# The normalization of three token groups in the first expert stage: on ScalarE instead of VectorE

## The chip, the cores and the metric

The kernel runs on one core of a Trainium2 chip. The metric is the device time of one execution in microseconds (us), the median over the runs. Below, PE is TensorE, DVE VectorE, ACT ScalarE, POOL GpSimd and SP SyncE, the names that the profile uses.

## What is computed

There are 16 sequences of 128 tokens with 128 features and a context of 77 rows per sequence. Four residual layers follow each other, each on the layer-normalized state:

```
x = x + tanh(g_xattn[0]) * attention(layernorm(x), ctx)            # one head
x = x + tanh(g_ffn[0])   * experts16(layernorm(x))  # top 4 of 16, and a shared one
x = x + tanh(g_xattn[1]) * attention(layernorm(x), ctx)            # 16 heads of 8
x = x + tanh(g_ffn[1])   * experts8(layernorm(x))   # top 2 of 8
layernorm(x) = (x - mean(x)) / sqrt(var(x) + 1e-5)
```

An expert is `silu(x @ gate) * (x @ up)`, weighted with the token's share for this expert, times a down matrix.

## The kernel before

All tokens lie in SBUF as `X`, token in the partition. The work runs over NG = 4 groups of GB = 4 sequences (GT = 512 tokens); a layer goes through the groups one after another, and a layer's first group is prepared inside the layer before it. I call the layers the set-up stage (with the first attention), the first expert stage (`mB`), the attention stage (`c_body`) and the last expert stage (`mD`). Every engine has its own program, written out in order by hand, and they meet only at semaphores.

To normalize a group, DVE takes the statistics of four sequences (`norm_stats`, L1043: `bn_stats` into `st`, `bn_aggr` into `mv`, then `ve` = variance + EPS at L1052). POOL raises `ve` to the power -1/2 (`inv_std`, L335: `rstd`). Then `norm_apply` writes `xn` = (X - mean) * rstd, one instruction per sequence; in the first expert stage and the last one DVE does it (L1054, L1059), in the attention stage POOL (L399, L404 and L407). The set-up stage has a form of its own: POOL also makes `shiftA` = -mean * rstd (L346), with `lessA` = -mean from DVE (L1084), and for three of its groups ACT writes `xn` as scale * X + bias (L832). PE transposes `xn` into the bank `Tb` (`norm_T`, L478), ACT copies it out as the high part `xh` (`norm_hi`, L822), and DVE subtracts the two for the low part `xl` (`norm_lo`, L1063).

Each expert stage has 8 units per group (`m.units`; in the first one a unit is two experts). For unit k of group g:

- PE (`m_up`, L551) computes gate and up in six matmuls into `S` banks. It runs two units ahead, and unit k waits until DVE has gated unit k-2 (L553, semaphore `t2`). `m_down` (L559) multiplies the weighted hidden rows `hb` by the down matrix.
- ACT (`m_silu`, L854) makes `sg` = silu(gate). It waits for PE's gate and for DVE's weighted unit k-2.
- DVE (`m_gated`, L1195) multiplies `sg` by up, and (`m_weighted`, L1200) by the tokens' weights `CR`, giving `hb`.
- SP (`weight_rows`, L294) writes the router's weights to memory once per group and loads them back, spread over the partitions, into a ring `CR` of four slots.

Around these units the bodies place the rest: in PE's body, for k = 0 the transposes of the next group, for k = 1 its router matmuls (L588, L589); in ACT's body `norm_hi` at k = 2 of the program (L902), the copy of the layer's result `ysb` at k = 1, and DMA issues of value pieces after each silu; in DVE's body (`m_body`, L1213) the router's steps at k = 2 to 5, `norm_stats` of the group after the next at k = 6 (L1243), and `norm_apply` of it at k = 7 (L1245). In the first expert stage this last call is made for three groups. DVE's program for groups 1 and 2 is a loop (L1317), ACT's is written out (L951). POOL's part of the stage is `inv_std` three times, at L434, L435 and L439; `split_up` (the up weights into high and low) and `expand_keys` for the attention stage stand behind the second and the third.

Of the kernel before, what the change touches and what calls it, by code (L numbers as in the profile page):

```python
# [79 lines left out]
def flamingo(nc, x, ctxT, ctx, w0, w4, gate_router, w13, w2, up, down, consts, out, comb_rows):  # L80
    with ExitStack() as stack:
        at = [16512]

        def sb(name, shape, dt=F32, offset=None):

            size = 4
            for n in shape[1:]:
                size *= n
            if offset is None:
                offset = at[0]  # L90
                at[0] += -(-size // 32) * 32
            place[name] = offset
            return nc.alloc_sbuf_tensor_at(name, shape, dt, offset=offset)
# [62 lines left out]
        mv = sb("mv", [P, GB, 2])  # L156
        ve = sb("ve", [P, GB])
        rstd = sb("rstd", [P, GB])
        mvA = sb("mvA", [P, 2, GB, 2])
        veA = sb("veA", [P, 2, GB])  # L160
        lessA = sb("lessA", [P, 2, GB])
# [57 lines left out]
        vs_zero, vx_rdy, wo_rdy = sem("vs_zero"), sem("vx_rdy"), sem("wo_rdy")  # L219
        sh_up, sh_silu, sh_hid, sh_hi, sh_lo = map(sem, ("sh_up", "sh_silu", "sh_hid", "sh_hi", "sh_lo"))  # L220
        w2s_hi, w2s_lo = sem("w2s_hi"), sem("w2s_lo")
        up_split, centred = sem("up_split"), sem("centred")
        stored = sem("stored")

# [100 lines left out]
        def _(pool):  # L325
# [9 lines left out]
            def inv_std(n):  # L335
                pool.wait_ge(var_rdy, n)
                nc.gpsimd.tensor_tensor(rstd[:], ve[:], mhalf[:], ALU.pow).then_inc(rstd_rdy, 1)  # L337

            def inv_stdA(n):
                par = n % 2  # L340
                pool.wait_ge(varA, n)
                if n > 2:
                    pool.wait_ge(xn_rdy, n - 2)
                nc.gpsimd.tensor_tensor(rstdA[:, par], veA[:, par], mhalf[:], ALU.pow).then_inc(powA, 1)
                wait_apart(pool, powA, n)
                nc.gpsimd.tensor_tensor(shiftA[:, par], lessA[:, par], rstdA[:, par], ALU.mult).then_inc(rstdA_rdy, 1)  # L346
# [84 lines left out]
                        inv_std(2 * NG + 3 + g)  # L431
                        norm_apply(2 * NG + 3 + g, (g + 2) % NG)

            inv_std(NG + 3)  # L434
            inv_std(NG + 4)  # L435
            pool.wait_ge(in_up, 96)
            for n in range(NG):
                split_up(n)
            inv_std(2 * NG + 1)  # L439
            pool.wait_ge(k_l, NG)  # L440
            expand_keys(0, 0, first=True)
            expand_keys(1, 1, first=True)
# [360 lines left out]
        def _(act):  # L803
# [46 lines left out]
            def keys_hi(g):  # L850
                act.wait_ge(k_mm, g + 1)
                A(kh[:, g * GS:(g + 1) * GS], bK[g][:, 0:GS], ACT.Identity, bias=cols[:, 2:3]).then_inc(k_h, 1)

            def m_silu(m, g, k):  # L854
                act.wait_ge(m.g_done, m.units * g + k + 1)
                if used(g, k):
                    act.wait_ge(m.h_done, START + m.units * g + k - 1)
                A(sg[:, k % 2, :], Gb[k % 2][:], ACT.Silu).then_inc(m.s_done, 1)  # L858
# [23 lines left out]
            def m_body(m, g, nxt, then=None, begun=0):  # L882

                for k in range(m.units):
                    if k >= begun:
                        m_silu(m, g, k)
                    if then:
                        then(k)
                    if k == 1 and used(g, 0):
                        m_y_copy(m, g - 1)  # L890
                    if k == 2 and m.shared:
                        act.wait_ge(sh_up, g + 1)
                        if used(g, 0):
                            act.wait_ge(sh_lo, g)
                        A(hs[:], Eb[64:P, :], ACT.Silu).then_inc(sh_silu, 1)
                    if k == 3 and m.shared:
                        act.wait_ge(sh_hid, g + 1)
                        if used(g, 0):
                            act.wait_ge(m.dn, START + m.units * (g - 1) + 5)
                        A(hst[0:64, :], hs[:], ACT.Copy).then_inc(sh_hi, 1)  # L900
                    if nxt is not None and k == 2:
                        norm_hi(nxt[0], xh[:, bass.ds(slot(nxt[2]), GT)])  # L902
                    if nxt is not None and nxt[1] is not None and k == 3:
                        m_route_act(nxt[1], nxt[2])
                    if nxt is not None and nxt[1] is not None and k == m.units - 3:
                        m_route_tanh(nxt[1], nxt[2])
                    if nxt is not None and nxt[1] is not None and k == m.units - 2:
                        m_route_copy(nxt[1], nxt[2])

            norm_hi(1, xf[:, 0])  # L910
            score_weights(2)
# [120 lines left out]
        def _(dve):  # L1032
# [10 lines left out]
            def norm_stats(n, g):  # L1043
                for t in range(GB):
                    i = V.bn_stats(st[:, t, :], xt(g, t))
                i.then_inc(stats, 1)
                wait_apart(dve, stats, n)
                for t in range(GB):
                    i = V.bn_aggr(mv[:, t, :], st[:, t, :])
                i.then_inc(aggr, 1)  # L1050
                dve.wait_ge(aggr, n)
                V.tensor_scalar(ve[:], mv[:, :, 1], EPS, None, ALU.add).then_inc(var_rdy, 1)  # L1052

            def norm_apply(n, g, first=False):  # L1054
# [158 lines left out]
            def m_body(m, g, nxt, then=None, stats_of=None, apply_next=True, begun=0):  # L1213

                for k in range(m.units):
# [26 lines left out]
                        route_weights(nm, ng)  # L1242
                    if stats_of is not None and k == m.units - 2:  # L1243
                        norm_stats(n + 1, stats_of)
                    if stats_of is not None and apply_next and k == m.units - 1:  # L1245
                        norm_apply(n + 1, stats_of)
                if then:
                    then(m.units)
# [229 lines left out]
```

## Time and profile before

| | |
|---|---|
| median of 3 runs | 322.72 us (322.35 to 323.2) |
| the profiled execution | 322.1 us, span 320.3 us |
| mean granted TensorE clock in it | 0.987 |
| PE, DVE, ACT, POOL busy | 89%, 74%, 41%, 27% of the span |
| instructions | 5453 |

The span is the time from the first to the last instruction of the core; the execution's own time also holds what lies around it. Busy shares are averages over all stages. The chain that ended last is followed back from the last instruction, at each step to what released it. In a timeline, a number in brackets is the time for which the engine had nothing to do ahead of the instruction, and behind the arrow stands what ended it.

### The profile page before, as it was taken

The page shows a single profiled execution, that of the slowest core. Times are in us where ns is not written, and L with a number is a line of the kernel's source. Part 1 is how long each engine was busy: PE and PEld are TensorE (multiplying, and loading weights), DVE is VectorE, ACT ScalarE, POOL GpSimd, SP SyncE. Part 2 cuts the span into 40 slices and gives each one's busy share as a digit, 9 for nine tenths or more (in the row PEclk, how much of TensorE's full clock was granted, in tenths as well). Part 3 has the DMA queues.
Part 4 walks back from the last instruction along what each step waited for, and adds up shares of the span by engine and source line. Part 5 has one row for each costly group of instructions (what it writes and reads, how often), then busy time and mean ns, then how long its engine had stood idle before and what let it go on. Part 6 is the DMA issues. An engine that isn't in the chain of part 4 may idle for free.

```text
span 320.3 us, 5453 instructions
## 1 busy us (share of the span) xinstructions
PE 283.6 (89%) x1646; PEld 210.7 (66%) x1646; DVE 237.1 (74%) x660; ACT 129.9 (41%) x275; POOL 87.7 (27%) x162
## 2 busy tenths in 40 slices
PE   6899689999899799488789789889889999999994
PEld 5688467666476465277677677768676676676661
DVE  2887979769989986557677686686748977778572
ACT  1587533242342332445454554554442332323320
POOL 8475310100650410733175165355110100100000
PEclk9999979999999999889999999999999999999999
DMA  6900164282341430000000000000024053231640
GB/s 225 337 21 0 37 222 148 54 242 67 102 156 46 132 123 33 0 2 0 2 1 2 0 2 3 0 0 3 0 86 158 25 190 75 106 125 35 210 154 33
DMA packets 15066, 25.26 MB, mean 79 GB/s; under 512 B 2341, under 2 KB 4339, under 8 KB 14835
## 3 DMA queue, kind: packets, MB, share of 16 engines
q1 hardware_dynamic: 12968, 23.88, 22.6%
q10 hardware_dynamic: 2072, 1.07, 1.2%
q8 instruction: 13, 0.21, 0.3%
q14 instruction: 13, 0.11, 0.1%
HBM read 22.98 MB, written 1.25 MB: 76 GB/s over the span
## 4 chain that ended last, share of the span: by engine, by line
PE 65%; issue 10%; DVE 9%; ACT 5%; DMA 5%; POOL 3%; SPq 2%; POOLq 0%; DVEq 0%; ACTq 0%
PE S L542 24%; PE Ybank L564 15%; PE Ybank L710 10%; PE S L687 2%; PE Tb L482 2%; DMA CR<-comb_rows 2%; DMA X<-in_x 2%; PE bank L697 2%; DVE xn L1059 2%; DMA comb_rows<-ct 1%; ACT pt L973 1%; PE Tb L674 1%; ACT PX L963 1%; SPq L307 1%; PE bank L580 1%
## 5 line engine op out<-in xcount | busy, mean ns | idle before, releaser
L858 ACT ACTIVATE sg<-S 128x512 f32<-128x512 f32 x64 | 38.0, 596 | 72.5 <-PE S L542 62.6
L1205 DVE TENSOR_TENSOR hb<-sg,CR 128x512 f32<-128x512 f32 x64 | 45.1, 705 | 13.0 <-issue 4.8
L337 POOL TENSOR_TENSOR rstd<-ve,mhalf 128x4 f32<-128x4 f32 x11 | 11.1, 1011 | 134.6 <-DVE ve L1052 134.6
L1198 DVE TENSOR_TENSOR sg<-sg,S 128x512 f32<-128x512 f32 x64 | 43.5, 680 | 5.7 <-ACT sg L858 3.5
L710 PE MATMUL Ybank<-VX,pt 128*128 128x128 f32 (+1 forms) x320 | 39.1, 277 | 6.7 <-ACT pt L973 6.7
L710 PEld LDWEIGHTS Ybank<-VX,pt 128*128 128x128 f32 (+1 forms) x320 | 37.1, 191 | 9.2 <-issue 9.1
L542 PE MATMUL S<-xh,WBH 128*128 128x512 f32 x64 | 33.3, 520 | 5.8 <-DVE sg L1198 3.0
L542 PE MATMUL S<-xh,UPH 128*128 128x512 f32 x64 | 36.1, 565 | 0.0
L564 PE MATMUL Ybank<-hb,W2T 128*128 128x512 f32 x64 | 33.0, 599 | 1.6 <-DVE hb L1205 1.6
L564 PE MATMUL Ybank<-hb,downw 128*128 128x512 f32 x64 | 33.0, 599 | 0.4 <-DVE hb L1205 0.4
L973 ACT ACTIVATE pt<-bank 128x512 f32<-128x512 f32 (+1 forms) x32 | 15.8, 494 | 35.4 <-PE bank L697 35.4
L1334 DVE TENSOR_REDUCE cmx<-S 128x8 f32<-128x616 f32 x32 | 25.4, 794 | 6.1 <-PE S L687 6.1
L963 ACT ACTIVATE PX<-PX 128x616 f32<-128x616 f32 x32 | 23.0, 720 | 11.3 <-DVE PX L1342 11.2
L1342 DVE TENSOR_TENSOR PX<-S,cmx 128x616 f32<-128x616 f32 x32 | 25.6, 800 | 1.1
L542 PE MATMUL S<-xh,WBL 128*128 128x512 f32 x64 | 25.5, 398 | 0.0
L542 PE MATMUL S<-xl,WBH 128*128 128x512 f32 x64 | 25.3, 395 | 0.0
L542 PE MATMUL S<-xh,UPL 128*128 128x512 f32 x64 | 25.2, 394 | 0.0
L542 PE MATMUL S<-xl,UPH 128*128 128x512 f32 x64 | 25.0, 391 | 0.0
L418 POOL COPY VX<-VS 128x36 f32 (+3 forms) x80 | 13.7, 220 | 41.0 <-PE Ybank L710 33.2
L542 PEld LDWEIGHTS S<-xh,WBH 128*128 128x128 f32 x64 | 12.0, 188 | 16.2 <-DVE sg L1198 9.0
L354 POOL TENSOR_TENSOR KT<-kk,CB 128x616 fp32r<-128x616 f32 x16 | 19.7, 1233 | 2.0 <-PE S L687 1.8
L542 PEld LDWEIGHTS S<-xl,UPH 128*128 128x128 f32 x64 | 12.1, 189 | 7.7 <-issue 6.2
(164 smaller groups left out, 513.2 us busy)
## 6 DMA issues: line engine op xcount, KB each, us to landing
CR<-comb_rows SPq DMA_DIRECT2D x64, 128.0 KB, 3.0
CR<-comb_rows SPq DMA_DIRECT2D x32, 256.0 KB, 3.5
w13raw<-in_w SPq DMA_DIRECT2D x1, 1088.0 KB, 10.9
X<-in_x SPq DMA_DIRECT2D x4, 256.0 KB, 6.1
upraw<-in_up SPq DMA_DIRECT2D x4, 256.0 KB, 3.9
out_x<-X SPq DMA_DIRECT2D x4, 256.0 KB, 3.4
cT<-in_ctxT SPq DMA_DIRECT2D x2, 308.0 KB, 5.6
CN<-in_ctx SPq DMA_DIRECT2D x1, 616.0 KB
```

Of the source, the lines that this page charges most:

```text
L354: nc.gpsimd.tensor_tensor(KT[:, par].rearrange("p a (h k) -> p a h k", h=HG), keys, heads, ALU.mult).then_inc(ks_done, 1)
L418: i = nc.gpsimd.tensor_copy(dst[:, :, j, h * HV:(h + m) * HV].rearrange("p u (i d) -> p u i d", i=m), src[:, :, j, 0:m])
L542: i = mm(dst, wp[:, col:col + P], xp[:, bass.ds(xs, GT)], start=n == 0, stop=n == 2)
L564: mm(Ybank[:, bass.ds(slot(g), GT)], m.wd[:, k, :], hb[:, k % 2, :], start=k == 0, stop=k == m.units - 1, skip_group_check=True).then_inc( ...
L710: i = mm(bO9[c // CU], pt[0:w, t % 2, c * P:(c + 1) * P], VX[0:w, t % 2, c, :], start=c % CU == 0, stop=c % CU == CU - 1)
L858: A(sg[:, k % 2, :], Gb[k % 2][:], ACT.Silu).then_inc(m.s_done, 1)
L963: A(p, p, ACT.Exp).then_inc(c_exp, 1)
L973: A(pt[:, t % 2, 4 * r * P:4 * r * P + w], bPa[r][:, 0:w], ACT.Copy).then_inc(c_ev, 1)
L1198: V.tensor_tensor(sg[:, k % 2, :], sg[:, k % 2, :], Ub[k % 2][:], ALU.mult).then_inc(m.t2, 1)
L1205: V.tensor_tensor(hb[:, k % 2, :], sg[:, k % 2, :], CR[:, k % RING, :], ALU.mult).then_inc(m.h_done, 1)
L1334: V.tensor_reduce(cmx[:, 2 * u:2 * u + 2, :], pair(u), AX, ALU.max, negate=True).then_inc(c_mx, 1)
L1342: V.tensor_tensor(PX[:, t % 2, u * UK:(u + 1) * UK].rearrange("p (s h k) -> p s h k", s=2, h=HG), pair(u), cmx[:, 2 * u:2 * u + 2, :].unsq ...
```

## The change

DVE's `norm_stats` also writes `less` = -mean. For three groups POOL forms `shift` = `less` * `rstd` behind the power (`inv_std_shift`). ACT's new `norm_applyB` writes `xn` as scale * X + bias in four activations, behind the silu of unit 7 and ahead of the silu of the next group's unit 0. DVE's `norm_apply` stays in the last expert stage only, and for the first stage's first transition (L1304), which is called apart.

```diff
--- before.py
+++ after.py
@@ -156,6 +156,8 @@
         mv = sb("mv", [P, GB, 2])
         ve = sb("ve", [P, GB])
         rstd = sb("rstd", [P, GB])
+        less = sb("less", [P, GB])
+        shift = sb("shift", [P, GB])
         mvA = sb("mvA", [P, 2, GB, 2])
         veA = sb("veA", [P, 2, GB])
         lessA = sb("lessA", [P, 2, GB])
@@ -219,6 +221,7 @@
         vs_zero, vx_rdy, wo_rdy = sem("vs_zero"), sem("vx_rdy"), sem("wo_rdy")
         sh_up, sh_silu, sh_hid, sh_hi, sh_lo = map(sem, ("sh_up", "sh_silu", "sh_hid", "sh_hi", "sh_lo"))
         w2s_hi, w2s_lo = sem("w2s_hi"), sem("w2s_lo")
+        shift_rdy = sem("shift_rdy")
         up_split, centred = sem("up_split"), sem("centred")
         stored = sem("stored")
 
@@ -335,6 +338,11 @@
             def inv_std(n):
                 pool.wait_ge(var_rdy, n)
                 nc.gpsimd.tensor_tensor(rstd[:], ve[:], mhalf[:], ALU.pow).then_inc(rstd_rdy, 1)
+
+            def inv_std_shift(n):
+                inv_std(n)
+                wait_apart(pool, rstd_rdy, n)
+                nc.gpsimd.tensor_tensor(shift[:], less[:], rstd[:], ALU.mult).then_inc(shift_rdy, 1)
 
             def inv_stdA(n):
                 par = n % 2
@@ -431,12 +439,12 @@
                         inv_std(2 * NG + 3 + g)
                         norm_apply(2 * NG + 3 + g, (g + 2) % NG)
 
-            inv_std(NG + 3)
-            inv_std(NG + 4)
+            inv_std_shift(NG + 3)
+            inv_std_shift(NG + 4)
             pool.wait_ge(in_up, 96)
             for n in range(NG):
                 split_up(n)
-            inv_std(2 * NG + 1)
+            inv_std_shift(2 * NG + 1)
             pool.wait_ge(k_l, NG)
             expand_keys(0, 0, first=True)
             expand_keys(1, 1, first=True)
@@ -851,6 +859,14 @@
                 act.wait_ge(k_mm, g + 1)
                 A(kh[:, g * GS:(g + 1) * GS], bK[g][:, 0:GS], ACT.Identity, bias=cols[:, 2:3]).then_inc(k_h, 1)
 
+            def norm_applyB(n, g):
+                act.wait_ge(shift_rdy, n - NG - 2)
+                act.wait_ge(xnT, n - 1)
+                for t in range(GB):
+                    i = A(xn[:, t * P:(t + 1) * P], X[:, g * GT + t * P:g * GT + (t + 1) * P], ACT.Identity,
+                          bias=shift[:, t:t + 1], scale=rstd[:, t:t + 1])
+                i.then_inc(xn_rdy, 1)
+
             def m_silu(m, g, k):
                 act.wait_ge(m.g_done, m.units * g + k + 1)
                 if used(g, k):
@@ -906,6 +922,8 @@
                         m_route_tanh(nxt[1], nxt[2])
                     if nxt is not None and nxt[1] is not None and k == m.units - 2:
                         m_route_copy(nxt[1], nxt[2])
+                    if nxt is not None and nxt[1] is mB and k == m.units - 1:
+                        norm_applyB(nxt[0] + 1, (nxt[2] + 1) % NG)
 
             norm_hi(1, xf[:, 0])
             score_weights(2)
@@ -1049,6 +1067,7 @@
                     i = V.bn_aggr(mv[:, t, :], st[:, t, :])
                 i.then_inc(aggr, 1)
                 dve.wait_ge(aggr, n)
+                V.tensor_scalar(less[:], mv[:, :, 0], -1.0, None, ALU.mult)
                 V.tensor_scalar(ve[:], mv[:, :, 1], EPS, None, ALU.add).then_inc(var_rdy, 1)
 
             def norm_apply(n, g, first=False):
@@ -1242,7 +1261,7 @@
                         route_weights(nm, ng)
                     if stats_of is not None and k == m.units - 2:
                         norm_stats(n + 1, stats_of)
-                    if stats_of is not None and apply_next and k == m.units - 1:
+                    if stats_of is not None and apply_next and m is mD and k == m.units - 1:
                         norm_apply(n + 1, stats_of)
                 if then:
                     then(m.units)
```

## Rows read from the trace of the kernel before

**Rows 1.** Page, section 4: the chain that ended last, by engine.

```profile
PE 65%; issue 10%; DVE 9%; ACT 5%; DMA 5%; POOL 3%; SPq 2%; POOLq 0%; DVEq 0%; ACTq 0%
```

**Rows 2.** List of waits, 40 to 130 us: total us, times, longest.

```profile
PE S L542 <- DVE sg L1198: 3.0, 2, 1.7
```

**Rows 3.** Timeline, border 2: start us, us, engine, line, what [idle before <- releaser].

```profile
81.75 0.60 ACT L858 ACTIVATE sg<-S 128x512 f32<-128x512 f32 x1 [0.81 <-PE S L542]
...
82.39 0.17 DVE L1052 TENSOR_SCALAR ve<-mv 128x4 f32<-128x4 f32 x1
...
82.64 1.01 POOL L337 TENSOR_TENSOR rstd<-ve,mhalf 128x4 f32<-128x4 f32 x1 [22.10 <-DVE ve L1052]
...
83.28 0.69 DVE L1205 TENSOR_TENSOR hb<-sg,CR 128x512 f32<-128x512 f32 x1
...
83.60 0.84 POOL L388 CAST UPH<-upraw 128x512 fp32r<-128x512 f32 x1
...
83.89 2.65 DVE L1059 TENSOR_SCALAR xn<-X,mv,rstd 128x128 f32 x4
...
85.86 0.60 POOL L388 CAST UPH<-upraw 128x512 fp32r<-128x512 f32 x1
86.46 0.67 DVE L1198 TENSOR_TENSOR sg<-sg,S 128x512 f32<-128x512 f32 x1
...
87.19 0.51 PE L542 MATMUL S<-xh,WBH 128*128 128x512 f32 x1 [1.38 <-DVE sg L1198]
```

**Rows 4.** Timeline, border 3.

```profile
105.33 0.17 DVE L1052 TENSOR_SCALAR ve<-mv 128x4 f32<-128x4 f32 x1
...
106.83 2.94 DVE L1059 TENSOR_SCALAR xn<-X,mv,rstd 128x128 f32 x4
...
110.41 0.50 PE L542 MATMUL S<-xh,WBH 128*128 128x512 f32 x1 [1.66 <-DVE sg L1198]
```

**Rows 5.** Timeline, border 1.

```profile
59.28 0.17 DVE L1052 TENSOR_SCALAR ve<-mv 128x4 f32<-128x4 f32 x1
...
60.09 0.69 DVE L1205 TENSOR_TENSOR hb<-sg,CR 128x512 f32<-128x512 f32 x1
...
60.69 1.11 DVE L1059 TENSOR_SCALAR xn<-X,mv,rstd 128x128 f32<-128x128 f32 x4
...
63.14 0.79 PE L542 MATMUL S<-xh,WBH 128*128 128x512 f32 x1
...
64.45 0.69 DVE L1205 TENSOR_TENSOR hb<-sg,CR 128x512 f32<-128x512 f32 x1 [2.05 <-DMA CR<-comb_rows]
...
67.82 0.39 PE L542 MATMUL S<-xl,WBH 128*128 128x512 f32 x1
...
68.05 0.40 PE L542 MATMUL S<-xh,WBL 128*128 128x512 f32 x1
...
69.07 0.25 PE L588 MATMUL Tb<-GW,xh 128*128 128x32 f32 x1 [0.62 <-DVE xl L1065]
```

**Rows 6.** Timeline, set-up stage: DVE, POOL and ACT rows of its normalization.

```profile
6.58 0.17 DVE L1083 TENSOR_SCALAR veA<-mvA 128x4 f32<-128x4 f32 x1 [0.16 <-DVE mvA L1078]
6.66 0.16 DVE L1084 TENSOR_SCALAR lessA<-mvA 128x4 f32<-128x4 f32 x1
...
9.04 1.04 POOL L344 TENSOR_TENSOR rstdA<-veA,mhalf 128x4 f32<-128x4 f32 x1 [0.67 <-DVE lessA L1084]
10.25 0.20 POOL L346 TENSOR_TENSOR shiftA<-lessA,rstdA 128x4 f32<-128x4 f32 x1 [0.18 <-POOL rstdA L344]
...
15.93 1.66 ACT L832 ACTIVATE xn<-X,shiftA,rstdA 128x128 f32<-128x128 f32 x4
17.47 0.59 ACT L848 ACTIVATE ptA<-S 77x512 f32<-77x512 f32 x1
```

**Rows 7.** PE at the end of the stage; PE's waits, 128 to 230 us.

```profile
129.53 1.10 PE L564 MATMUL Ybank<-hb,W2T 128*128 128x512 f32 x2 [1.62 <-DVE hb L1205]
...
PE Tb L482 <- POOL xn L407: 1.6, 3, 0.5
```

## Prediction

> **What bounds the kernel now.** I read the page's busy shares and the chain that ended last first [rows 1]: PE holds 65% of the chain and DVE 9%, so a saving on DVE counts only where PE waits for it. The list of waits for 40 to 130 us then says where that is in the first expert stage: twice, 3.0 us together, PE's `S` matmuls sit idle until DVE's `sg` (the gated product) is there [rows 2]. The timelines place both at the borders between token groups. I write (g,k) for unit k of group g, and border g for the passage from group g-1 to group g.
>
> At border 2 the statistics' last step `ve` starts at 82.39, POOL's power runs from 82.64 to 83.65, and the four `xn` instructions of DVE take 2.65 us. The gated product (2,0) ends at 87.13 only, and PE starts unit (2,2) at 87.19 after 1.38 us of idle time [rows 3]. At border 3 the same four take 2.94 us (POOL is at its key expansion then), and PE starts at 110.41 after 1.66 us [rows 4]. At border 1 they take 1.11 us, the plain cost, and PE does not wait at 63.14. There the late thing is a transfer: hb(1,0) stands 2.05 us until a `CR` row has landed, at 64.45, and PE later waits 0.62 us for `xl` before the router's matmuls at 69.07 [rows 5]. So what the change takes from DVE is on the path at borders 2 and 3, not at border 1.
>
> **What the change does, part by part.**
>
> *Removed:* three times four `xn` instructions on DVE, 1.11 + 2.65 + 2.94 = 6.70 us of its queue [rows 3 to 5]. They carry one semaphore increment each time, and no DMA moves with them.
>
> *Added on POOL:* three products `shift` = `less` x `rstd`, each behind its power. The set-up stage has this pair already: a power from 9.04 to 10.08, the product at 10.25 for 0.20 [rows 6], so 0.17 of waiting and 0.20 of work. Behind it on POOL stand `split_up` and `expand_keys`, which start some 0.4 us later; PE needs neither soon, since the keys and the up weights serve the next two stages.
>
> *Added on ACT:* three times four activations. The set-up stage's four took 1.66 us (15.93 to 17.59), and the next activation began at 17.47, 0.12 before their end [rows 6]. What counts is where they stand: behind silu(g-1,7) and ahead of silu(g,0), so silu(g,0), which ran early before the change (81.75 at border 2) [rows 3], cannot start until the power, the product and the four passes are done. DVE's gated product (g,0) waits for that silu, and PE's unit (g,2) waits for the gated product. The normalization therefore leaves DVE but not the chain into PE. Identity with a scale is already used in this stage for `ysb`, so I cost a table load at nothing.
>
> *Added on DVE:* `less` ahead of `ve` in every `norm_stats`. Two such instructions start 0.08 apart (6.58 and 6.66) [rows 6]; I take 0.08 for each where DVE's order is on the path. The upper bound is a whole instruction, 0.17.
>
> *Border 2.* `ve` moves to 82.47 and ends 82.64; the power starts 0.08 later as now, 82.72 to 83.73; the product could run 83.90 to 84.10. Beside it DVE runs hb(1,7), now at 83.28, then 83.36 to 84.05. Does that hold the product up? The row to judge by is POOL's cast at 83.60: beside hb it took 0.84, and 0.60 without it at 85.86 [rows 3]. So there is a cost of up to 0.24. The power, though, ran 1.01 across the start of the same hb, and hb itself took its usual 0.69. I take a delay of the product to the end of hb: 84.05 to 84.25. ACT starts 0.08 later, 84.33 to 85.99, silu(2,0) at 85.87 for 0.60 to 86.47, the gated product 0.03 later (an estimate, below POOL's 0.08) for 0.67 to 87.17, PE 0.06 later as now, at 87.23. Against 87.19 that is +0.04.
>
> The Trainium skill, in "SBUF — State Buffer", section "SBUF: two separate sides", has DVE instructions with two SBUF inputs and GpSimd instructions contend for an exclusive lock that the first comer holds for its whole length. By that rule the product waits for the end of hb, the +0.04; with no lock it would be -0.11. The cast's row agrees, and hb's undisturbed 0.69 inside the power does not.
>
> *Border 3.* The same spacing applies, because hb(2,7) stands as far behind `ve`: PE starts 87.23 - 82.39 = 4.84 behind the old start of `ve`, so 105.33 + 4.84 = 110.17 against 110.41: -0.24. The bounds are -0.39 without the delay and 0 if POOL's key expansion, or something else, costs ACT's passes as much again.
>
> *Border 1.* 59.28 + 4.84 = 64.12; hb(0,7) stands 0.81 behind `ve` here and hb(1,7) 0.89 at border 2, so I use 64.04. PE now starts at 63.14 [rows 5], so unit (1,2) comes 0.9 later. What hides it is the transfer: hb(1,0) waits until 64.45 anyway. The delay runs on through PE's queue to the last matmul of unit (1,3), 68.05 before, 68.95 then; the router's matmuls can follow 0.23 behind it, as the last two matmuls of the unit do (67.82 and 68.05) [rows 5], at 69.18 against 69.07: +0.1. If that cover is gone, it costs 0.9.
>
> *`less` on the path.* At the end of this stage PE waits 1.62 for hb, behind the statistics: +0.08. In the attention stage PE waits for POOL's `xn` three times [rows 7], each behind `norm_stats`: 3 x 0.08 = +0.24. In the last stage PE has no wait on DVE behind the statistics: DVE waits for weight rows there, which hides it. The bounds of this term are 0 and 4 x 0.17 = 0.68.
>
> *Sum:* +0.1 + 0.04 - 0.24 + 0.08 + 0.24 = +0.22 us. It is made against the profiled execution, 322.1 us (span 320.3, 1.8 around it), which stands 0.6 under the median of 322.72. So I expect a profiled 322.3 and a median of 322.9. The time that DVE loses from its queue is found again as its wait for silu(g,0).
>
> **The rivals.**
>
> *A, faster: DVE's stretched passes were the whole wait.* If PE's two waits of 1.38 and 1.66 vanish and the small terms stay (0.1 + 0.08 + 0.24), the change is -2.6: 320.1. For it: the waits name DVE's `sg`, and ACT sat idle 0.81 before silu(2,0) [rows 2, 3]. Against it: silu(g,0) stands behind the passes in ACT's order, and the power plus the product alone end near 84.2. It needs ACT to have the four passes done about 1.4 sooner than rows 6 allow. The Trainium skill, "Perfetto Trace Analysis", section "Optimizing Scalar/DVE Operations", says that moving work to Scalar may make sense where DVE is saturated; taken as a forecast that is this rival. The trace agrees on DVE's load at the borders only. Chance 0.09.
>
> *B, slower: silu held back at border 1 with no cover.* Unit (1,2) starts 0.9 late, and if the `CR` transfers land no later than about 64.0, or PE's wait for `xl` moves along with the transposes and `xh`, the 0.9 stands instead of 0.1: +0.22 + 0.8 = +1.02; 322.7 + 1.0 = 323.7. For it: PE had nearly no gap there, and shared gate, transposes, `xh` and `xl` all follow in one row. Against it: 2.05 of DVE's waiting for the transfer and 0.62 of PE's [rows 5]. It decides from the point where `xh` comes later than DVE is free for `xl`. Chance 0.2.
>
> *C, slightly faster:* ACT's passes run unhindered and `less` hides: -0.11 at border 2, -0.39 at border 3, +0.1 at border 1: -0.4, 322.3. It counts as no change. Chance 0.15.
>
> *D, a partly relieved border:* one of the two waits goes whole, about -1.3: 321.4. Nothing in the rows asks for it. Chance 0.06.
>
> **How the numbers follow.** The forecast, 322.9, has 0.5. About 0.3% (1 us) is what a measurement of this kernel can tell from no change. Forecast and C lie within it, and a fifth of B's chance as well, but the upper bound of `less` and of the delays puts 0.06 of the forecast beyond it: 0.63 for no change, 0.15 for faster (A and D), 0.22 for slower. The range runs from 322.0 (C with its terms at their bounds) to 324.0 (B, a little over its centre); A, D and the far bounds together, about 0.2, are left out.
>
> **What the changed profile would show.** DVE idle before `sg`(g,0), released by ACT's `sg`, some 2 us at borders 2 and 3; ACT's four `xn` at about 1.65 us, starting some 1.9 behind the start of `ve`; PE starting unit (g,2) 4.7 to 4.9 behind the old `ve`, with 1.4 us idle still. At border 1 PE idles 0.9 before unit (1,2), while the router's matmuls stand about where they stood. In the attention stage POOL's power stands 0.08 later behind the batch-norm aggregate. The forecast is wrong if PE's idle time at borders 2 and 3 shrinks below 0.8 (A or D), if the router's matmuls of group 2 move by over 0.5 against the first unit of the stage (B), or if ACT's passes take other than 1.65, or a table load appears.

## The result, and the profile after

In the first comparison the changed kernel took 325.23 us (median of 6 runs, 324.18 to 326.39) against 322.85 us (6 runs, 321.52 to 323.2): ratio 1.0106, 95% interval 1.0067 to 1.0144. The forecast was 322.9 and its range ended at 324.0. The profiled execution took 326.1 us with a span of 324.3; before, 322.1 and 320.3. Here and below, a median is over all runs of a kernel, while a ratio and its interval leave out the runs that lie over 1.5% above that kernel's fastest.

The page of the changed kernel, its busy times and the row of PE's clock:

```profile
PE 285.9 (88%) x1646; PEld 212.4 (66%) x1646; DVE 231.0 (71%) x659; ACT 133.9 (41%) x287; POOL 87.8 (27%) x165
...
PEclk9999999989999999659999999999999999999999
```

DVE lost 6.1 us of work, ACT gained 4.0, and PE's busy time grew by 2.3 with the same 1646 matmuls. Matmuls that last longer are a matter of PE's clock. First, though, what I had forecast at border 2 ((g,k) is unit k of group g; border g is the passage from group g-1 to group g), in the changed kernel's timeline:

```profile
83.46 0.17 DVE L1070 TENSOR_SCALAR less<-mv 128x4 f32<-128x4 f32 x1
83.54 0.16 DVE L1071 TENSOR_SCALAR ve<-mv 128x4 f32<-128x4 f32 x1
...
83.78 1.01 POOL L340 TENSOR_TENSOR rstd<-ve,mhalf 128x4 f32<-128x4 f32 x1 [23.61 <-DVE ve L1071]
...
84.35 0.69 DVE L1224 TENSOR_TENSOR hb<-sg,CR 128x512 f32<-128x512 f32 x1
...
84.97 0.20 POOL L345 TENSOR_TENSOR shift<-less,rstd 128x4 f32<-128x4 f32 x1 [0.18 <-POOL rstd L340]
...
85.20 0.49 ACT L866 ACTIVATE xn<-X,shift,rstd 128x128 f32<-128x128 f32 x1 [2.34 <-POOL shift L345]
...
86.75 1.06 ACT L874 ACTIVATE sg<-S 128x512 f32<-128x512 f32 x2
...
87.36 0.69 DVE L1217 TENSOR_TENSOR sg<-sg,S 128x512 f32<-128x512 f32 x1 [2.32 <-ACT sg L874]
...
88.10 0.50 PE L550 MATMUL S<-xh,WBH 128*128 128x512 f32 x1 [0.70 <-DVE sg L1217]
```

The chain is the one forecast: `less` and `ve` 0.08 apart, power, product, passes from 85.20, silu at 86.75, and DVE now idle 2.32 us for ACT where it was busy before. PE starts 88.10 - 83.46 = 4.64 us behind the first instruction after the statistics, forecast 4.84, before 4.80 [rows 3].

Where the time went is easiest to see from a mark that both kernels have: POOL's power, once per group. In the changed kernel:

```profile
37.62 1.01 POOL L340 TENSOR_TENSOR rstd<-ve,mhalf 128x4 f32<-128x4 f32 x1 [8.33 <-DVE ve L1071]
58.79 1.01 POOL L340 TENSOR_TENSOR rstd<-ve,mhalf 128x4 f32<-128x4 f32 x1 [17.01 <-DVE ve L1071]
83.78 1.01 POOL L340 TENSOR_TENSOR rstd<-ve,mhalf 128x4 f32<-128x4 f32 x1 [23.61 <-DVE ve L1071]
107.25 1.01 POOL L340 TENSOR_TENSOR rstd<-ve,mhalf 128x4 f32<-128x4 f32 x1 [13.35 <-DVE ve L1071]
129.46 1.01 POOL L340 TENSOR_TENSOR rstd<-ve,mhalf 128x4 f32<-128x4 f32 x1 [10.48 <-DVE ve L1071]
165.84 1.02 POOL L340 TENSOR_TENSOR rstd<-ve,mhalf 128x4 f32<-128x4 f32 x1 [5.13 <-DVE ve L1071]
```

The second power belongs to border 1, the third to border 2, the fourth to border 3. Differences of these starts are the distances d1 to d5: 21.17, 24.99, 23.47, 22.21, 36.38. Before, the powers start at 36.97, 59.53, 82.64, 105.58, 128.22 and 161.92: 22.56, 23.11, 22.94, 22.64, 33.70. So the changed kernel won 1.39 in d1, lost 1.88 in d2, 0.53 in d3, won 0.43 in d4 and lost 2.68 in d5, where the change hardly touches anything. The five distances behind d5 differ by 0.07 at most.

The windows of both kernels show why. Columns: stretch, its length, then busy time of PE, PE's loads, DVE, ACT and POOL, granted TensorE clock, DMA share, GB/s. Before:

```profile
42.00:48.00 6.00, 6.00 (x23) 4.54 (x21) 3.89 (x7) 2.49 (x5) 0.00 (x0) 0.72 0.72 223
...
66.00:75.00 9.00, 8.38 (x39) 5.81 (x38) 6.98 (x17) 3.71 (x7) 0.00 (x0) 1.00 0.63 185
...
132.00:138.00 6.00, 3.23 (x26) 2.95 (x27) 4.15 (x6) 2.69 (x4) 4.08 (x8) 0.72 0.00 0
```

The changed kernel:

```profile
36.00:60.00 24.00, 21.30 (x89) 14.93 (x87) 22.05 (x69) 8.71 (x16) 5.01 (x6) 1.00 0.49 140
...
69.00:75.00 6.00, 5.64 (x21) 4.18 (x22) 4.42 (x9) 1.28 (x3) 0.00 (x0) 0.72 0.33 115
...
132.00:147.00 15.00, 11.07 (x86) 9.80 (x82) 6.90 (x9) 6.73 (x10) 6.02 (x14) 0.54 0.00 1
```

0.50 is 1.2 GHz and 1.00 is 2.4 GHz; a mean of 0.72 over 6 us is some 3.4 us at the lower level. I call such a piece a low stretch. The kernel before has a low stretch at 42 to 48 us, behind PE's pause at 39 to 41, and one behind its pause of 3.37 us at the start of the attention stage. The changed kernel has none at 42, one at 70, behind two pauses at border 1 (0.46 and 1.16 us), and at the start of the attention stage, behind a pause of the same length, one of 14 us instead of 3.4. The rows, first of the kernel before, then of the changed one:

```profile
67.04 0.69 DVE L1205 TENSOR_TENSOR hb<-sg,CR 128x512 f32<-128x512 f32 x1 [1.30 <-issue]
134.77 1.40 PE L687 MATMUL S<-KT,qq 32*128 32x308 f32 x16 [3.37 <-DVE PX L1342]
```

```profile
63.20 0.47 PE L550 MATMUL S<-xh,WBH 128*128 128x512 f32 x1 [0.46 <-DVE sg L1217]
67.33 0.69 DVE L1224 TENSOR_TENSOR hb<-sg,CR 128x512 f32<-128x512 f32 x1 [2.52 <-issue]
69.36 0.25 PE L596 MATMUL Tb<-GW,xh 128*128 128x32 f32 x1 [1.16 <-DVE xl L1084]
136.18 1.40 PE L695 MATMUL S<-KT,qq 32*128 32x308 f32 x16 [3.36 <-DVE PX L1361]
```

The distances d1 and d5 follow the low stretches, not the instructions that were moved. In d2 a second thing counts. DVE's hb(1,1) stands idle with no releaser shown ("issue"); of the semaphores it waits for in the program only that of its own `CR` row can still be open then, so it is most likely this row that is late (an inference). DVE makes `xl` behind hb(1,1), and PE's router matmuls wait for `xl`. In the changed kernel hb(1,1) starts 8.54 us behind the second power, before 7.51. This start explains 1.0 of the 1.88 us in d2, the low stretch the rest. Either the change brings other low stretches, or one profile of each kernel caught them in other places. The experiments are about that.

### The profile page after: what moved, and what is told of

Read it like the earlier page. It is cut to its first block, busy times and chain, and to the rows that moved or that the text cites. A ratio compares the mean times of both kernels' runs of the same rounds, so it can differ in the third digit from the quotient of the medians.

```text
span 324.3 us, 5470 instructions
## 1 busy us (share of the span) xinstructions
PE 285.9 (88%) x1646; PEld 212.4 (66%) x1646; DVE 231.0 (71%) x659; ACT 133.9 (41%) x287; POOL 87.8 (27%) x165
## 3 DMA queue, kind: packets, MB, share of 16 engines
HBM read 22.98 MB, written 1.25 MB: 75 GB/s over the span
## 4 chain that ended last, share of the span: by engine, by line
PE 60%; DVE 11%; issue 10%; ACT 6%; DMA 6%; POOL 3%; SPq 2%; ACTq 1%; POOLq 0%; DVEq 0%
PE S L550 20%; PE Ybank L572 13%; PE Ybank L718 10%; DMA CR<-comb_rows 3%; PE S L695 2%; PE Tb L490 2%; DMA X<-in_x 2%; PE bank L705 2%; DVE sg L1217 2%; DVE hb L1224 1%; DMA comb_rows<-ct 1%; PE bank L588 1%; PE Tb L682 1%; ACT pt L991 1%; SPq L310 1%
## 5 line engine op out<-in xcount | busy, mean ns | idle before, releaser
L718 PE MATMUL Ybank<-VX,pt 128*128 128x128 f32 (+1 forms) x320 | 41.3, 287 | 6.3 <-ACT pt L991 6.3
L718 PEld LDWEIGHTS Ybank<-VX,pt 128*128 128x128 f32 (+1 forms) x320 | 39.1, 200 | 9.0 <-issue 8.8
L705 PE MATMUL bank<-CB,PX 128*128 128x128 f32 x96 | 17.3, 291 | 0.0
```

The costliest lines, as they stand in the source:

```text
L705: i = tr(bP[r][0:w, c % 4 * P:c % 4 * P + P], PX[:, t % 2, chunk_col(c):chunk_col(c) + w], I)
L718: i = mm(bO9[c // CU], pt[0:w, t % 2, c * P:(c + 1) * P], VX[0:w, t % 2, c, :], start=c % CU == 0, stop=c % CU == CU - 1)
```

## The experiments

Every ratio below is to runs of the kernel before that were made together with the kernel named; four executions above 340 us are left out of what I count and of the medians by clock. Where distances or windows are given, they are those of the one profiled execution of that kernel.

**The small work alone.** Statistics and POOL as in the change, all passes on DVE; DVE also waits for POOL's product before it overwrites `less`:

```diff
-                    if nxt is not None and nxt[1] is mB and k == m.units - 1:
-                        norm_applyB(nxt[0] + 1, (nxt[2] + 1) % NG)
...
-                    if stats_of is not None and apply_next and m is mD and k == m.units - 1:
+                    if stats_of is not None and apply_next and k == m.units - 1:
```

> Only the change's small work: less on DVE, the shift product on POOL, the passes stay on DVE. Theory S (the small work costs): about +1 us or more over the kernel before. Theory C (the loss is TensorE's granted clock in stretches that the moved passes bring about): within 0.5 us of before, mean clock about 0.987. Theory W (ACT's order and the DMA issues behind it make units wait): also within 0.5 us of before, since nothing moved.

323.99 us against 323.36, ratio 1.0022 (0.996 to 1.0085). Distances 22.67, 22.93, 22.98, 22.65, 34.01: d1 to d4 are those of before. The median is 0.6 us above the kernel before, a little more than the 0.5 that I had allowed, with an interval that includes 1. The 31 runs of before ran from 319.88 to 326.85, at mean clocks from 0.928 to 0.989. The three runs that I had seen before the prediction lay within 0.9 us of each other; this kernel scatters over seven.

**Border 1 alone, and borders 2 and 3 alone.**

```diff
-                    if nxt is not None and nxt[1] is mB and k == m.units - 1:
+                    if nxt is not None and nxt[1] is mB and nxt[0] == NG + 2 and k == m.units - 1:
...
-                    if stats_of is not None and apply_next and m is mD and k == m.units - 1:
+                    if stats_of is not None and apply_next and not (m is mB and isinstance(g, int)) and k == m.units - 1:
```

The other kernel has `nxt[0] > NG + 2` and `(m is mD or isinstance(g, int))` there, and POOL makes `shift` only where ACT needs it.

> ACT normalizes at border 1 alone, DVE at borders 2 and 3. Theory C: if the low stretch at 70 to 75 us comes from border 1, it is here too, the distance between the second and third power on POOL is about 25 us (23.1 before), and the stretch at 42 to 48 us may come or not independently of it. Theory W: border 1 costs 1 to 1.2 us by the later CR rows, total +1. Forecast theory (the delay is hidden by the transfer): +0.1.

323.94 us, ratio 1.0027 (0.9982 to 1.0073). Distances 21.20, 24.94, 23.45, 22.64, 33.88, with a low stretch at 70 to 75 us and hb(1,1) 8.74 behind the second power: so far this spoke for border 1 as the cause.

> ACT normalizes at borders 2 and 3, DVE at border 1. Theory C: the result hangs on the clock's stretch at the start of the attention stage, 3 to 4 us long as before (then -0.3 to -0.5 in all) or 13 us long as in the changed kernel (then +2.3). Theory W: border 2 costs 0.5 and border 3 gives back 0.4, total 0.

322.71 us, ratio 0.9981 (0.9937 to 1.0024). Its profile is of its slowest run (328.17 us) and has three low stretches, one of them at 72 to 76 us with border 1 on DVE (hb(1,1) at 8.91), and still d4 = 22.21, the gain at border 3.

**Matmuls without use in the pause at the start of the attention stage.** They write a bank that nothing reads any more, and change no result. The same edit was put into the changed kernel and into the one before:

```diff
                     c_scores(0, 0)
+                    pe.wait_ge(x_done, START + 2 * NG - 1)
+                    for _ in range(12):
+                        mm(Eb[:], WBH[:, 0:P], xh[:, 0:GT], start=True, stop=True)
```

> The changed kernel with twelve matmuls without use put into PE's pause at the start of the attention stage. Theory C: the long low stretch (132 to 145 us) goes or shortens to at most 4 us, the distance from the fifth to the sixth power falls from 36.4 to 33.7 or less, and the total by 2.5 to 3 us to 322.5 or less. Theories S and W: no gain, the total stays at 325 or rises with the added matmuls.

321.55 us, ratio 0.9935 (0.99 to 0.9971), mean clock 0.993. The windows of this kernel:

```profile
69.00:75.00 6.00, 5.75 (x23) 4.18 (x23) 4.25 (x9) 1.17 (x3) 0.00 (x0) 0.72 0.31 108
132.00:141.00 9.00, 7.51 (x69) 5.99 (x66) 6.81 (x9) 5.69 (x9) 5.25 (x9) 1.00 0.00 0
```

The stretch at 132 is gone and d5 is 32.54 instead of 36.38. The one at 70 stays.

> The kernel before with the same twelve matmuls without use at the start of the attention stage. Theory C: the low stretch there goes here too, -1 to -2 us (about 321.5 beside 323.4), and then the kernel before and the changed one with these matmuls (321.55) agree within 0.3%. Theory W: the changed one with them stays 1% above this one.

319.55 us, ratio 0.9922 (0.9885 to 0.996). Its profile has no low stretch in either stage: d1 to d5 are 21.10, 23.64, 22.92, 22.61, 32.49. That gives the price of a stretch in each place: 22.56 - 21.10 = 1.5 us at 42, 33.70 - 32.49 = 1.2 us at 135, and 36.38 - 32.54 = 3.8 us for the long one. In all nine profiles of this document with the twelve matmuls d5 is 32.49 to 32.55, in the eleven without them 33.40 to 36.38.

I had expected the two kernels with these matmuls to agree within 0.3%. Their medians, 319.55 and 321.55, are 0.6% apart; they were not run together, and their ratios to the kernel before are 0.9922 and 0.9935. All 11 runs of this one have a mean clock of 0.992 or more, 6 of 10 of the other.

**The changed kernel again.** No edit.

> The changed kernel once more, beside the kernel before, on this job's chip. Theory C (clock): in both kernels the time follows the run's mean granted clock, about 2 us for each 0.01, and runs of the two kernels at the same mean clock lie within 0.7 us of each other; any difference of the medians comes from how often the low stretches come. Theory W (the moved passes cost work on the path): runs of the changed kernel lie 1 us or more above runs of the kernel before at the same mean clock.

324.73 us, ratio 1.0072 (1.0029 to 1.0115): a second time slower, by an interval that leaves out 1. Runs of equal mean clock lie together here: at 0.982, the changed kernel 323.06 (2 runs) and the one before 323.19. Only 2 of its 11 runs lie at 0.985 or above, against 11 of 29 before.

**silu(g,0) ahead of the passes.** ACT's order at the border is turned round:

```diff
                     if k >= begun:
                         m_silu(m, g, k)
+                    if m is mB and g > 0 and k == 0:
+                        norm_applyB(NG + g + 2, (g + 1) % NG)
...
-                    if nxt is not None and nxt[1] is mB and k == m.units - 1:
-                        norm_applyB(nxt[0] + 1, (nxt[2] + 1) % NG)
```

> As the changed kernel, but ACT takes silu(g,0) ahead of the four normalization passes. Theory order (silu held back by the passes is what kept the gain away): PE's waits at borders 2 and 3 before unit (g,2) go from 0.7 and 1.2 us to 0.3 or less, the distances between the powers at these borders fall by 1 to 1.5 us each, total about -2 to -2.5 us against the changed kernel. Rival (the wait passes on to the CR rows or to silu(g,1)): under -0.5 us.

321.87 us, ratio 0.9974 (0.9928 to 1.0021). Distances 22.59, 23.31, 22.24, 20.92, 33.52: d3 is 0.7 and d4 1.7 below the kernel before. PE's waits from 36 to 132 us in this kernel, all of them:

```profile
PE S L550 <- DVE kk L1144: 2.7, 1, 2.7
PE Ybank L572 <- DVE hb L1224: 1.7, 1, 1.7
PE Tb L596 <- DVE xl L1084: 1.3, 2, 0.8
PE Tb L602 <- DVE combB L1209: 1.2, 1, 1.2
```

and of the changed kernel, where `sg` is still among them with 2.4 us in three waits:

```profile
PE S L550 <- DVE kk L1144: 2.7, 1, 2.7
PE S L550 <- DVE sg L1217: 2.4, 3, 1.2
PE Ybank L572 <- DVE hb L1224: 1.7, 1, 1.7
PE Tb L596 <- DVE xl L1084: 1.6, 2, 1.2
```

With silu first the wait for `sg` is gone and the time at borders 2 and 3 with it. That is the mechanism on which the forecast rested, shown from its other side: it was ACT's order that kept the gain away there, not the passes. Border 1 gains nothing: d2 is 23.00 to 24.22 in the four profiles with silu first, none of which has a low stretch at 70.

> silu(g,0) first and the twelve matmuls at the start of the attention stage together. If order and clock are independent, the gains add: about 320 or below, 1% under the kernel before. If the clock's stretches only move to another place, 321.5 as with the matmuls alone.

Both edits: 319.26 us (6 runs), ratio 0.9879 (0.9798 to 0.9959), distances 22.72, 24.05, 22.02, 20.78, 32.55. That agrees with the gains adding, though the interval is wide; a low stretch at 42 is there.

**The parts once more, with the twelve matmuls.**

> ACT normalizes at border 1 alone, with the twelve matmuls without use at the start of the attention stage in place, which keep that stretch out of the comparison. If border 1 brings the low stretch at about 70 us and the moved passes nothing else: this run's median lies 1 us or more above the kernel before with the same twelve matmuls (319.55), near 321 to 321.5, and its profile shows the stretch at 70 to 75 us. If the stretch comes by chance whichever engine normalizes: about 319.6 to 320.

321.61 us, ratio 0.997 (0.9934 to 1.0007). The profile has border 1 on ACT and no low stretch from 42 us on:

```profile
42.00:48.00 6.00, 5.83 (x30) 4.65 (x31) 5.11 (x10) 2.90 (x5) 0.00 (x0) 1.00 0.67 220
69.00:75.00 6.00, 6.00 (x25) 4.00 (x26) 4.74 (x14) 1.43 (x4) 0.00 (x0) 1.00 0.37 124
```

d2 and d3 are 22.82 and 22.92, against 23.11 and 22.94 before, with hb(1,1) only 7.06 us behind the second power. So in this execution the passes at border 1 cost nothing, and they do not always bring the stretch at 70. The profile is not what I expected, but the median is: 321.61 lies where I had put it for the case that border 1 costs. At mean clocks of 0.992 to 0.995 the nine runs of this kernel have a median of 321.58, the six of `before_fill` 319.90. They were not run together, and the profiled run is one of the quickest, so a cost of border 1 in the other runs is not ruled out.

> ACT normalizes at borders 2 and 3 alone, with the twelve matmuls. From the distances of the powers, border 3 gives back 0.43 and border 2 nothing, the attention stage costs 0.2: 319.4. If the changed kernel's loss comes with these borders, 321 or more.

321.49 us, ratio 0.9972 (0.9933 to 1.001); profile at clock 1.0 with d3 = 22.91 and d4 = 22.18. The distances came as expected, the median did not: 5 of its 12 runs lie at mean clocks of 0.986 to 0.989 and take 323, those at 0.995 take 320.0 (3 runs).

**Five more matmuls without use** ahead of the router's matmuls at border 1 of the changed kernel, into the wait of 1.2 to 1.5 us:

```diff
                     if k == 1 and route_next:
+                        if m is mB and g == 1:
+                            pe.wait_ge(m.y_cp, START + 1)
+                            for _ in range(5):
+                                mm(Ybank[:, 0:GT], WBH[:, 0:P], xh[:, GT:2 * GT], start=True, stop=True)
                         m_logits(nxt[1], nxt[2])
```

> The changed kernel with the twelve matmuls, and five more without use put ahead of the router's matmuls at border 1, into PE's wait of 1.2 to 1.5 us for xl. Theory C: the low stretch at 70 to 75 us goes, the distance from the second to the third power falls from 25 us to 23 to 23.6, the mean clock is 0.998 or more and the median 319.3 to 319.8 instead of 321.55. Rival (the long distance there is the wait for the CR rows, not the clock): 321 to 322, as without the five.

322.32 us, ratio 0.998 (0.9935 to 1.0025). The stretch at 70 is absent, but this profile has one of about 7 us at 41 to 48 (d1 = 23.92), and d2 stays long at 24.97 with no low clock in it. For d2 this speaks for the rival of the expectation, the wait for the `CR` rows: hb(1,1) stands 9.30 us behind the second power, the latest of all profiles, and the five matmuls and PE's remaining wait of 0.78 us fill the gap that this leaves.

**Twelve more in the pause at 39 to 42 us**, with silu first:

```diff
             m_up(m, 0, 1, ring=False)
+            pe.wait_ge(k_l, 1)
+            for _ in range(12):
+                mm(Ybank[:, 0:GT], WBH[:, 0:P], xh[:, 0:GT], start=True, stop=True)
             pe.wait_ge(k_l, 2)
```

> silu(g,0) first, the twelve matmuls at the start of the attention stage, and twelve more in PE's pause of 2.7 us at 39 to 42 us. If the low stretch at 42 to 48 us goes without another coming at border 1: 1.4 us for the first distance between powers, of which the transfers at border 1 give back up to 0.5, total about 318 to 318.5. If the stretch only moves to 70 us: 319.3 or more.

318.43 us, ratio 0.9881 (0.9845 to 0.9918), and the profiled execution has a span of 315.1 with no low stretch after the start:

```profile
36.00:75.00 39.00, 38.35 (x160) 27.14 (x159) 31.69 (x89) 15.95 (x31) 5.19 (x6) 1.00 0.51 157
132.00:141.00 9.00, 7.01 (x65) 5.71 (x63) 6.26 (x12) 5.26 (x10) 2.94 (x7) 1.00 0.01 2
```

This is the lowest median of all versions, 1.2% below the kernel before; the matmuls without use alone took that kernel down by 0.8%.

**Both kernels with both sets of matmuls.**

> The kernel before with twelve matmuls without use in each of PE's two long pauses (39 to 42 us, and the start of the attention stage). Clock theory: mean clock 0.995 or more in most runs, median 319 to 319.6.

320.14 us, ratio 0.992 (0.9891 to 0.9948), median clock 0.998. The clocks came as expected, the time is 0.5 us above my range: the second set brought nothing over the first.

> The changed kernel with the same two sets of matmuls. Clock theory: as before_fill2 within 0.3%, 319.2 to 319.9, where its mean clock is as high; at border 3 it gives back 0.4, in the attention stage it loses 0.2. If the moved passes themselves cost the 0.7 to 1.1%: 321.5 to 322.5 at the same clock.

320.65 us, ratio 0.9943 (0.9911 to 0.9974), median clock 0.997, and also above my range. With both pauses filled the two kernels differ by 0.2%, with intervals that overlap. The 1.06% is not there. Both profiles still have a low stretch at 33 to 39 us, ahead of the first pause, and d1 is as long with it (22.51 and 22.42) as with one at 42.

**The kernel before, and the changed kernel, as they are.**

> The kernel before as it is. Clock theory: its runs at a mean clock of 0.985 or more make up about half (44 of 95 so far), median 322.7 to 323.4.

323.84 us, ratio to its own other runs 1.004 (1.0002 to 1.0078): the same kernel, and an interval that leaves out 1. Three of its 11 runs lie at 0.985 or more, where I had expected about half. Its profile shows what I had taken for the mark of the change, a long wait for `xl` (hb(1,1) at 8.86) and the low stretch at 70:

```profile
69.00:75.00 6.00, 5.66 (x21) 4.28 (x22) 4.56 (x10) 1.26 (x3) 0.00 (x0) 0.72 0.32 113
...
69.34 0.26 PE L588 MATMUL Tb<-GW,xh 128*128 128x32 f32 x1 [2.12 <-DVE xl L1065]
```

Distances 21.11, 25.07, 23.43, 22.65, 33.71: d1 to d3 are those of the changed kernel in the first comparison (21.17, 24.99, 23.47), to within 0.1.

> The changed kernel as it is. If it has low stretches more often: at most 2 of 12 runs at 0.985 or more, median 324.5 to 325.5. If the earlier runs fell so by chance: about half of them at 0.985 or more, and the median within 0.3% of the kernel before.

323.13 us, ratio 1.0017 (0.9977 to 1.0058), 4 of 12 runs at 0.985 or more: the median came as expected for chance, the share lies between the two expectations. Here the changed kernel shows d1 to d3 as the one before did: 22.64, 22.81, 22.93, with a low stretch at 42 to 48, none at 70 and hb(1,1) at 6.89:

```profile
42.00:48.00 6.00, 4.54 (x16) 3.49 (x16) 3.73 (x10) 1.28 (x3) 1.09 (x3) 0.72 0.68 207
69.00:75.00 6.00, 6.00 (x29) 4.30 (x28) 5.06 (x9) 2.51 (x6) 0.00 (x0) 1.00 0.67 212
132.00:147.00 15.00, 11.06 (x87) 9.78 (x86) 6.93 (x10) 6.90 (x10) 6.29 (x14) 0.66 0.00 1
```

> The changed kernel as it is, once more. If the first comparison fell so by chance: 4 or more of 12 runs at a mean clock of 0.985 or more, ratio to the kernel before between 0.998 and 1.004. If the change brings low stretches: at most 2 of 12 there, ratio 1.006 or more.

323.83 us, ratio 1.0022 (0.998 to 1.0064), 3 of 12 runs at 0.985 or more: the ratio is as for chance, the share between the two expectations.

> silu(g,0) ahead of the normalization, once more. The distances between the powers gave 0.8 us at border 2 and 1.75 at border 3, less 0.2 in the attention stage: ratio about 0.993 to 0.996 with the clock's scatter on top; distances again near 22.1 and 20.8. If the first result was the clock's chance: ratio about 1.

322.00 us, ratio 0.9975 (0.9935 to 1.0015), between the two expectations; d3 = 22.31 and d4 = 21.11 are 0.2 and 0.3 above what I expected and keep most of the gain. Over both times the median of silu first is 321.87 us (24 runs) against 323.10 (164 runs), -0.38%; a rough interval drawn from the runs alone is -0.53 to -0.12%.

## All runs by clock

The median time of the runs in each band of mean clock, over all jobs (number of runs in brackets):

| mean clock | kernel before | changed kernel | silu first |
|---|---|---|---|
| 0.970 to 0.975 | 325.86 (12) | 326.04 (9) | 324.07 (3) |
| 0.975 to 0.980 | 324.46 (34) | 324.73 (12) | 321.99 (8) |
| 0.980 to 0.985 | 323.19 (44) | 323.32 (11) | 322.01 (6) |
| 0.985 to 0.990 | 322.11 (62) | 321.83 (8) | 320.40 (3) |

Changed and before lie within 0.3 us in every band, silu first 1.2 to 2.5 us below. Over all executions the medians are 323.10 (164 runs) and 323.97 (41), +0.27%, and +0.14% without the first six; a rough interval for the first, drawn from the runs alone, is +0.06 to +0.54%. A line through the runs above 0.95, with the first six left out, gives 2.6 us for each 0.01 of mean clock and -0.03 us for the change.

What stays open is whether the change moves runs toward the lower bands. 72 of 164 runs of the kernel before lie at 0.985 or above, 9 of 41 of the changed one, 7 of its last 24. If both kernels had the same share, nine or fewer of 41 would come up in about 1 case of 100, and seven or fewer of 24 in about 1 of 8. The second count leaves out the 17 runs that raised the question. The bands cannot answer it, since they compare runs at a clock that the change itself may have lowered. Two more counts, made after the fact, point to the change. Take the kernels with border 1 on ACT and no matmuls without use (the changed one, border 1 alone, silu first). In each of the four sets of runs made together that hold such kernels, fewer of their runs lie at 0.985 or above than of the kernel before: 1 of 10 against 11 of 31, 5 of 23 against 11 of 29, 4 of 12 against 19 of 46, and 6 of 24 against 9 of 23. And with the twelve matmuls all 11 runs of the kernel before lie at 0.99 or above, of the changed one 6 of 10, of borders 2 and 3 alone 7 of 12, of border 1 alone 10 of 12 (and 6 of 12 of the changed one with the five more matmuls). With both sets of matmuls all runs of both kernels do. So a real cost of some 0.1 to 0.5%, by way of the clock, is likely but not shown; 1.06% is more than the later runs bear out.

The long stretch at 132 us stood in two of four profiles of the changed kernel, in the one of borders 2 and 3 alone, and in neither profile of the kernel before. These are too few, and what decides its length was not found. The stretch at 70 us goes with a late hb(1,1): it stands in seven of the nine profiles in which hb(1,1) starts 8.5 us or more behind the second power, in none of the other eleven, and of the two exceptions one has the five matmuls in the gap. Late starts occur with border 1 on DVE (8.86 and 8.91, of seven profiles without silu first) and on ACT (six of nine, 8.54 to 9.30). Whether the passes at border 1 help to make this row late is open.

## Why the prediction was wrong, point by point

**The sum held where it can be read.** The table sets the terms against distances of profiles that have the same clock in that stretch and, for border 1, an hb(1,1) at most 7.5 us behind the second power.

| term | forecast | measured |
|---|---|---|
| border 1 | +0.1 | -0.3 to 0 (d2 22.82 and 22.81 against 23.11 and 22.93, d3 the same) |
| border 2 | +0.04 | 0 (d3 22.92 and 22.93 against 22.94 and 22.92); 23.3 to 23.5 in seven other profiles, with the passes on ACT and on DVE, not explained |
| border 3 | -0.24 | -0.43 (d4 22.17 to 22.21 in every kernel with it and ACT's order as in the change, 22.61 to 22.65 in every one without) |
| `less`, attention stage | 3 x 0.08 | 3 x 0.06 (24.93, 24.92 and 22.74 became 24.99, 24.98 and 22.81), and 0.05 at its start |

The measured terms come to about -0.2 to -0.5, the forecast to +0.22. Both are no change, and in the bands of equal clock the runs of the kernels without added matmuls show none.

**The step that failed** is the one that made the sum against one profiled execution and said that "about 0.3% (1 us) is what a measurement of this kernel can tell from no change". The profile's row of PE's clock has dips, its windows at 42 to 48 and 132 to 138 us are at 0.72, and I did not read them. A low stretch costs 1.2 to 3.8 us by its place and length, and two or three of them come and go between executions of one kernel. That term was taken as zero. In the first comparison the changed kernel's six runs lie at mean clocks of 0.971 to 0.982, where the kernel before takes 323.2 to 325.9 us; the forecast stood on a profile at 0.987. So nearly all of the 2.4 us between the medians is this term, and the range had no room for it. That all six runs fell so low was bad luck, at least in part; whether the change had a share in it is the open question above. With 1 us for what a measurement can tell I also gave "no change" 0.63 and cut the range at +1.3.

**Border 1** began as forecast: PE's unit (1,2) was late, and DVE's hb(1,0) waited for its `CR` row 0.46 us where it had waited 2.05 [rows 5]. PE's idle time ahead of the unit was 0.46 and not 0.9. The forecast then followed PE's queue to the router's matmuls. Their start is set elsewhere, by hb(1,1) and the `xl` behind it, and hb(1,1) has a wait of its own, 1.30 us in the trace of the kernel before already, which I had not looked at. It moves from one execution to the next: hb(1,1) starts 6.9 to 9.3 us behind the second power, and d2 is that plus 15.6 to 16.8 in all twenty profiles. PE's wait for `xl` is 1.16, 1.33 and 1.48 us in three profiles of the changed kernel and does not occur in the fourth; it is 0.62, 2.12 and 1.31 in three with the passes on DVE (`before`, `before_again`, `before_fill`). Rival B, that the delay at this border decides, had this wait among its conditions. It is not at work in the changed kernel's profile with d2 of 22.81, and it is not ruled out as a reason for late rows in the others.

**Border 2.** The product on POOL was not delayed to the end of hb: it ran at 84.97 for its plain 0.20, 0.18 behind the power as in the set-up stage, and 0.07 ahead of hb's end (hb ran from 84.35 to 85.04). The +0.15 for it, at borders 2 and 3, was one term too many, and explains most of border 3's 0.43 against 0.24. At border 2 PE also starts sooner behind the power, by 4.32 us against 4.55, but d3 does not show it; why was not found. The Trainium skill's rule of the exclusive lock, "SBUF — State Buffer", section "SBUF: two separate sides", is not borne out by these small instructions: hb starts inside POOL's power (83.78 to 84.79) and takes its usual 0.69. The product's overlap of 0.07 us alone would be thin evidence. The rule may still be behind the drawn-out casts of [rows 3].

**Rival A**, by which DVE's stretched passes were the whole wait, was near on the price and wrong about the change: with silu first, 0.7 and 1.7 us come back. In the changed kernel PE's waits at borders 2 and 3 fell from 1.38 and 1.66 to 0.70 and 1.21. The 0.70 is below the 0.8 that I had named as a sign against the forecast, but it is not the change's: the unchanged kernel has 0.69 there in `before_again`, where PE came late out of the stretch at 70, and the changed kernel 1.20 in `after_again2`, where there was none. Like for like the waits fell to 1.2 each.

## What to carry to other kernels

Read the granted clock over the stages before summing against one profile, and look at the scatter of some ten runs or more before saying what a measurement can tell; where runs differ by clock, compare them in bands of equal clock. When a step is moved to an idle engine, look at what stands behind it in that engine's order: here the passes had room on ACT, and the silu behind them had not. Where PE has a pause of 3 us, matmuls without use in it can be worth more than the work that was moved.

## What was not expected of the hardware

The mean granted clock of one unchanged kernel ran from 0.928 to 0.998 over its executions on the same chips, and its time from 319.8 to 328.6 us. A comparison of it with itself gave an interval that left out 1 (1.004, 1.0002 to 1.0078), and so did two of four with the changed kernel, which is as fast at equal clock (1.0106 and 1.0072). Low stretches came behind pauses of 3.4 and 2.7 us, in some executions and not in others, and also behind PE's wait for `xl`: seven of the eight profiles in which it was 1.16 to 2.17 us have one at 70, the eighth, `before_fill` with 1.31 us, has none. Most low stretches in these windows were about 3.4 us long; those of 7 us (at 41 to 48, and one at 132) and of 10 to 14 us at the start of the attention stage, where PE's work is itself broken by waits, are the exceptions.
